# A new order of the steady batch on four engines, with odd layouts for denominators and block maxima

## The reference

```python
h = layernorm(x) * (1 + ca) + sa
x = x + ga * attention(h)            # 16 heads of 64, causal
h = layernorm(x) * (1 + cb) + sb
x = x + gb * ffn(h)                  # silu(gate) * up, then down, 352 hidden

# attention, per head
s = (q * scale) @ k.T
p = where(causal, 0, exp(s - max(s)))       # the max is taken before the mask
out = (p @ v) / (sum(p) + 1e-8)
# every ffn linear first rounds input and weight to FP4 in blocks of 16
scale = max(max(abs(block)) / 6, 1e-12)
q = GRID[searchsorted(MID, abs(block / scale))] * sign * scale
```

## Time and profile before

| | us |
|---|---|
| median of 3 runs | 1282.47 (1282.1 to 1282.92) |
| the profiled execution | 1283.31 |
| its span, first to last instruction | 1281.7 |
| mean granted TensorE clock | 0.993 of full |

### The profile page before, as it was taken

How to read it: one execution, slowest core, us unless ns; L and a number is a source line. 1 busy time by engine, 2 the same in 40 slices (tenths; PEclk the granted TensorE clock), 3 DMA queues, 4 the chain that set the end, 5 groups by cost and what they waited for, 6 DMA issues and landing times.

```text
span 1281.7 us, 34320 instructions
## 1 busy us (share of the span) xinstructions
PE 1247.3 (97%) x10194; PEld 1023.0 (80%) x10194; DVE 987.8 (77%) x2465; ACT 900.1 (70%) x2992; POOL 847.8 (66%) x1586
## 2 busy tenths in 40 slices
PE   6999999999999999999999999999999999999995
PEld 4778888888888888888888888788888788888774
DVE  5577877778777778777778777778787778787767
ACT  6676767776767777777777677777667777667761
POOL 4757666677666677666667666667666667666672
PEclk9999999999999999999999999999999999999997
DMA  3000000000000000000000000000000000000000
GB/s 105 20 20 24 18 7 23 23 23 23 13 9 23 23 23 22 10 13 23 23 23 21 9 15 23 23 23 21 6 18 23 23 23 20 6 18 23 19 21 9
DMA packets 38936, 26.53 MB, mean 21 GB/s; under 512 B 2912, under 2 KB 34144, under 8 KB 38912
## 3 DMA queue, kind: packets, MB, share of 16 engines
q1 hardware_dynamic: 38496, 25.96, 7.0%
q10 hardware_dynamic: 416, 0.26, 0.1%
HBM read 21.94 MB, written 4.28 MB: 20 GB/s over the span
## 4 chain that ended last, share of the span: by engine, by line
PE 95%; ACT 2%; DVE 2%; issue 1%; POOL 0%; DMA 0%; DVEq 0%; POOLq 0%
PE ps_m L1183 25%; PE ps_s L1282 20%; PE ps_m L1157 18%; PE ps_o L1312 14%; PE ps_m L1235 9%; PE ps_s L1292 5%; PE ps_m L1259 3%; ACT probs L688 1%; ACT qk L646 0%; PE ps_m L1403 0%; PE ps_s L1259 0%; ACT probs_t L642 0%; DMA x_in<-L_attn_x 0%; DVE neg_max L925 0%; DVE qy L62 0%
## 5 line engine op out<-in xcount | busy, mean ns | idle before, releaser
L688 ACT ACTIVATE probs<-ps_s,neg_max 128x128 f32<-128x128 f32 (+1 forms) x1024 | 424.2, 433 | 182.2 <-PE ps_s L1292 180.6
L467 POOL TENSOR_SCALAR probs<-probs,r_den 128x256 f32<-128x256 f32 (+1 forms) x768 | 355.4, 479 | 0.0
L925 DVE TENSOR_REDUCE neg_max<-ps_s 128x4 f32<-128x1024 f32 x256 | 305.6, 1215 | 61.0 <-PE ps_s L1282 61.0
L465 POOL TENSOR_TENSOR probs<-probs,r_den 128x128 f32<-128x128 f32 x256 | 107.5, 420 | 307.5 <-DVE r_den L936 293.3
L1282 PE MATMUL ps_s<-qk 64*128 64x256 f32 x2048 | 264.9, 394 | 1.8 <-ACT probs L688 1.8
L642 ACT COPY probs_t<-ps_m 128x512 f32<-128x512 f32 x287 | 167.8, 605 | 117.8 <-PE ps_m L1157 117.7
L1157 PE MATMUL ps_m<-ident,probs 128*128 128x128 f32 x1524 | 233.9, 277 | 5.4 <-ACT qk L646 3.6
L1282 PEld LDWEIGHTS ps_s<-qk 64*128 64x128 f32 x2048 | 183.0, 187 | 61.5 <-issue 32.4
L688 ACT ACTIVATION_READ_ACCUMULATOR probs<-ps_s,neg_max 128x1 f32 x1024 | 220.9, 216 | 0.0
L1157 PEld LDWEIGHTS ps_m<-ident,probs 128*128 128x128 f32 x1524 | 170.9, 140 | 38.0 <-ACT qk L646 13.3
L1312 PE MATMUL ps_o<-probs_t,v 128*64 128x256 f32 x2016 | 191.6, 332 | 0.7
(11 more groups left out here) (161 smaller groups left out, 1803.7 us busy)
## 6 DMA issues: line engine op xcount, KB each, us to landing
mod_a<-mod_rows SPq DMA_DIRECT2D x32, 256.0 KB, 3.3
x_res<-L_attn_x SPq DMA_DIRECT2D x32, 128.0 KB, 2.1
x_in<-L_attn_x SPq DMA_DIRECT2D x31, 128.0 KB, 2.1
out<-y_out SPq DMA_DIRECT2D x31, 128.0 KB, 1.8
mod_b<-mod_rows SPq DMA_DIRECT2D x31, 64.0 KB, 2.9
wkv<-L_attn_Wkv SPq DMA_DIRECT2D x3, 256.0 KB, 5.7
wo<-L_attn_Wo SPq DMA_DIRECT2D x1, 512.0 KB, 5.0
wkv<-L_attn_Wkv SPq DMA_DIRECT2D x2, 128.0 KB, 3.5
```

The lines of the kernel that those rows point to most:

```text
L465: nc.gpsimd.tensor_tensor(cols, cols, r_den[:, u % 4, 0:1].to_broadcast([P, P]), ALU.mult)
L467: ins = nc.gpsimd.tensor_scalar(cols, cols, r_den[:, u % 4, s:s + 1], 1.0, ALU.mult, ALU.mult)
L688: ins = nc.scalar.activation(probs[:, u % 4, h, t * P:(1 + 2 * t) * P], ps_s[:, 2 * (u % 2) + h, t * N:t * N + (1 + t) * P], ACT.Exp, bias ...
L925: nc.vector.tensor_reduce(neg_max[:, u % 4, :], ps_s[:, 2 * (u % 2):2 * (u % 2) + 2, :].rearrange("p b (t j) -> p (b t) j", t=2), AX.X, AL ...
```

## The change

Nothing is computed otherwise, but in another order and in part in other layouts. Each quarter's list changes on every engine:

- `SHARED`: some steps change places within their quarter. `v` number 2 goes from quarter 1 to 2, `down` number 0 and `hqt` number 1 from 2 to 3. There are still 36 steps, in three banks in turn.
- TensorE: masks stand at other places; after every `values` a mask comes first.
- ScalarE takes `t1` of quarter 0 and `t1` of quarter 1 and the `o_t` copy of quarter 3; VectorE takes `t1` of quarter 3 and the `o_t` copy of quarter 2.
- VectorE: the denominators of units 7 (of the batch before), 0 and 6 stand later in their quarters, `input_stats` in quarter 1.
- GpSimd: `keep` first in quarter 0, `residual` first in quarter 1, the second `round_hidden` at the end of quarter 2, `modulate` first in quarter 3.
- `den` has 9 columns per unit and `den_eps` 6; the eps addition reads 3 pairs with a stride of 3 and writes 6 columns. The hidden rows' block maxima are written in 11 pairs with a stride of 3 (`pair_scales`).
- The layer-norm result is made by `tensor_scalar` with two pointers in place of `scalar_tensor_tensor` with a broadcast second input.
- `den` is set to 1.0 by GpSimd at the start, and ScalarE waits for all eight set-up instructions before its first DMA.

```diff
+def pair_scales(nc, step, src, blocks, amax, scale, inverse):
+    pairs = amax[:, :].rearrange("p (a b) -> p a b", b=3)[:, :, 0:2]
+    step(nc.vector.tensor_reduce(pairs, src.rearrange("p (a b k) -> p a b k", b=2, k=BLOCK), AX.X, ALU.max,
+                                 apply_absolute_value=True))
+    step(nc.vector.tensor_scalar(scale[:, 0:blocks].rearrange("p (a b) -> p a b", b=2), pairs, 1.0 / 6.0, 1e-12,
+                                 ALU.mult, ALU.max))
+    step(nc.vector.reciprocal(inverse[:, 0:blocks], scale[:, 0:blocks]))
...
         SHARED = (
-            (("xqt", 2, 0), "t0", "qk0", "t1", "qk1", ("gate", 2, 0), ("v", 0, 0), ("v", 0, 1), "t2", ("up", 2, 0), ("gate", 2, 1)),
-            ("t0", "qk0", "qk1", ("up", 2, 1), ("wo", 1, 0), "t1", ("wo", 1, 1), ("hqt", 2, 0), "t2", ("v", 0, 2)),
-            (("hqt", 2, 1), ("down", 2, 0), "qk0", "t0", "qk1", "t1", ("v", 0, 3), ("xt", -1, 0), "t2"),
-            ("t0", "qk0", "qk1", ("down", 2, 1), "t1", "t2"))
+            ("t0", ("xqt", 2, 0), "qk0", "qk1", "t1", ("gate", 2, 0), ("v", 0, 0), ("up", 2, 0), ("v", 0, 1), "t2", ("gate", 2, 1)),
+            ("t0", "qk0", ("up", 2, 1), ("wo", 1, 0), "t1", ("wo", 1, 1), "qk1", "t2", ("hqt", 2, 0)),
+            ("qk0", "t0", ("v", 0, 2), "t1", "qk1", "t2", ("v", 0, 3), ("xt", -1, 0)),
+            ("qk0", ("hqt", 2, 1), "t0", "t1", ("down", 2, 0), ("down", 2, 1), "t2", "qk1"))
...
+            init(nc.gpsimd.memset(den[:, :, :], 1.0))
...
                 for j in range(PAIRS):          # GpSimd
                     if j == 0:
+                        keep()
                         normalize(i, -1)
                         normalize(i, 0)
                     elif j == 1:
-                        keep()
+                        residual()
                         normalize(i, 1)
-                        residual()
                         round_hidden(i - 2, 0)
                         normalize(i, 2)
-                        round_hidden(i - 2, 1)
                     elif j == 2:
+                        input_rstd()
                         attended_rstd()
-                        input_rstd()
                         normalize(i, 3)
                         normalize(i, 4)
+                        round_hidden(i - 2, 1)
+                    elif j == 3:
                         modulate()
-                    elif j == 3:
                         normalize(i, 5)
                         normalize(i, 6)
                         round_ffn_in()
...
+            act.wait_ge(pool_setup, POOL_SETUP)
             act.dma_start(x_in[:, :, :], x_v[0]).then_inc(x_loaded, 16)
...
-                    nc.vector.scalar_tensor_tensor(dst[t], src[:, t, :], mv[:, t, 0:1], r[:, t:t + 1].to_broadcast([P, P]),
-                                                   ALU.subtract, ALU.mult).then_inc(ready, 1)
+                    nc.vector.tensor_scalar(dst[t], src[:, t, :], mv[:, t, 0:1], r[:, t:t + 1], ALU.subtract, ALU.mult).then_inc(ready, 1)
...
-                    nc.vector.tensor_scalar(den_eps[:, u % 4, :], den[:, u % 4, :], SOFTMAX_EPS, None,
+                    nc.vector.tensor_scalar(den_eps[:, u % 4, :].rearrange("p (a b) -> p a b", b=2),
+                                            den[:, u % 4, :].rearrange("p (a b) -> p a b", b=3)[:, :, 0:2], SOFTMAX_EPS, None,
```

More of the change, by code:

```diff
@@ L178, in adaln_block @@
         qm = [sb(f"qm{n}", [P, I]) for n in range(3)]
-        amax = [sb(f"amax{n}", [P, I // BLOCK]) for n in range(3)]
+        amax = [sb(f"amax{n}", [P, 3 * I // BLOCK // 2]) for n in range(3)]
         scale = [sb(f"scale{n}", [P, I // BLOCK]) for n in range(3)]
@@ L734, in body @@
                         shared_reads(shared, j, 0)
[L735 removed]
                         shared_reads(shared, j, 1)
                         shared_reads(shared, j, 2)
+                        exponentials(6, 1)
                         exponentials(7, 0)
                         exponentials(7, 1)
[L740 to L741 removed]
+                        shared_reads(shared, j, 7)
+                        shared_reads(shared, j, 6)
+                        out_copy()
             high_parts(0)
@@ L984, in body @@
                         maxima(0)
-                        denominators(-1)
-                        shared_reads(0, 0)
-                        shared_reads(0, 3)
                         maxima(1)
@@ L990, in body @@
                             low_parts(2)
+                        out_copy()
+                        denominators(-1)
+                        shared_reads(0, 1)
                         shared_reads(0, 5)
-                        denominators(0)
-                        shared_reads(0, 8)
-                        shared_reads(0, 9)
-                        out_copy()
+                        shared_reads(0, 7)
                         hidden_scales(i - 2, 0)
                         shared_reads(0, 10)
+                        denominators(0)
@@ L998, in body @@
                     elif j == 1:
-                        denominators(1)
                         maxima(2)
                         maxima(3)
+                        denominators(1)
+                        input_stats()
                         hidden_magic(i - 2, 0)
+                        shared_reads(1, 2)
                         shared_reads(1, 3)
                         hidden_scales(i - 2, 1)
-                        shared_reads(1, 4)
+                        shared_reads(1, 5)
                         denominators(2)
-                        shared_reads(1, 6)
+                        if i_is(i, 1):
+                            shared_reads(1, 8)
+                    elif j == 2:
@@ L1008, in body @@
                         hidden_magic(i - 2, 1)
-                        if i_is(i, 1):
-                            shared_reads(1, 7)
-                    elif j == 2:
-                        input_stats()
+                        denominators(3)
+                        maxima(4)
                         attended_stats()
-                        maxima(4)
                         maxima(5)
-                        denominators(3)
-                        if i_is(i, 1):
-                            shared_reads(2, 0)
+                        out_copy()
@@ L1327, in body @@
                         at_place(0, 0)
+                        mask(0, 1)
                         at_place(0, 1)
-                        mask(0, 1)
                         at_place(0, 2)
@@ L1334, in body @@
                         at_place(0, 6)
+                        mask(1, 0)
+                        mask(1, 1)
                         at_place(0, 7)
                         at_place(0, 8)
-                        mask(1, 0)
-                        mask(1, 1)
                         at_place(0, 9)
@@ L1361, in body @@
                         at_place(2, 2)
+                        mask(5, 0)
                         at_place(2, 3)
                         at_place(2, 4)
-                        mask(5, 0)
+                        mask(5, 1)
                         at_place(2, 5)
-                        mask(5, 1)
                         at_place(2, 6)
                         at_place(2, 7)
-                        at_place(2, 8)
                     elif j == 3:
                         mask(6, 0)
-                        mask(6, 1)
                         at_place(3, 0)
                         at_place(3, 1)
+                        mask(6, 1)
+                        mask(7, 0)
                         at_place(3, 2)
+                        mask(7, 1)
                         at_place(3, 3)
-                        mask(7, 0)
                         at_place(3, 4)
-                        mask(7, 1)
                         at_place(3, 5)
+                        at_place(3, 6)
+                        at_place(3, 7)
             shared = shared_steps(-1)
-            for place in ((2, 7), (3, 1), (3, 2)):
+            for place in ((2, 7), (3, 0), (3, 7)):
                 kind, b, k, bank, _ = shared[place]
```

74 lines of the change are left out of this document (37 added, 37 removed).

## The result

The changed kernel is slower: a median of 1299.55 us (four runs, 1299.04 to 1299.78) against 1282.28 for the kernel before in the same comparison. The ratio is 1.0131, its 95% interval 1.0118 to 1.0145. The forecast was 1271.3 with a range of 1247 to 1290, so sign and range are both missed.

A forecast was written before the change was run, and what follows sets the result against it. TensorE's list plus its gaps bound the kernel: 1.25 us a batch out, 0.8 in, so 30 x 0.45 = 13.5 off 1283.31, start 2.35 on, 1272.2, adjusted by 0.84 to the median, 1271.3; range 1247 to 1290.

The forecast's parts named there:

- The removal: TensorE's waits in a steady batch: the new order takes out all of them, 1.25 us a batch.
- the nine gaps: TensorE's losses per batch: slow first scores block 0.3, four idle times 0.67 in all, four smaller ones 0.28.
- Step 3: Small new waits at quarter 0's second `v`, `xt` and unit 5's scores: 0 to 0.5 us a batch, taken as 0.25.
- step 1: Quarter 3, feed-forward input: `xq` comes late for `xqt` through `h2` and denominators 6; loss 0 to 0.4 us, taken as 0.3.
- step 2: Quarter 1, first transpose: waits for unit 0's late denominators and normalisation; 0 to 0.5 us, taken as 0.25.
- Step 5: Two-pointer normalising instructions on VectorE: 0.25 us each (bounds 0.175 to 0.83), 1 us less a batch on VectorE.
- Rival E: Two-pointer instructions wait for GpSimd: four take 1.9 us, `xt` up to 0.6 late, +0.15 a batch, 1289.3; chance 0.08.
- Rival D: Quarter 3: denominators 6 end later than 8.95 us into it, delaying `xqt`; 0.45 a batch longer, 1298.3; chance 0.12.
- Step 4: Odd layouts of denominators and hidden maxima avoid VectorE's wait for GpSimd; mostly off the path, 0 to 0.3 us a batch.
- Step 6: Start: ScalarE's first input DMA waits for eight set-up instructions and is issued at 3.1; +2.35 us (1.5 to 2.5).
- Step 7: SP: the output store and `mod_b` load move behind a later `y_out`; costs nothing.
- the tail: The end of the kernel: same hand-written end, change 0, within 1 us either way.

The follow-up runs named there:

- Experiment 15: As experiment 13, plus the first quotient instruction moved into VectorE's idle time and one hidden rounding instruction into GpSimd's; 1258.98 us, ratio 0.9814.
- experiment 12: As experiment 10, with GpSimd's second hidden rounding and modulation ahead of its normalisation of unit 4; 1280.29 us, ratio 0.9968.
- experiment 6: Changed kernel with GpSimd holding its second hidden rounding until both tiles of the next input are normalised; 1302.70 us, ratio 1.0144.
- experiment 5: Kernel before with only the two-pointer form of the four normalising instructions; 1282.02 us, ratio 0.9982.
- Experiment 4: Changed kernel with the old scalar_tensor_tensor in place of the two-pointer tensor_scalar; 1314.76 us, ratio 1.0248.
- experiment 10: Experiments 1 and 3 combined, with two quarter 3 reads ahead of the quotients, denominators 6 before the last read, keep behind unit 7; 1274.79 us, ratio 0.9930.
- experiment 11: As experiment 10, with one rounding instruction of the second hidden half moved into GpSimd's idle time in quarter 2; 1274.33 us, ratio 0.9925.
- experiment 13: As experiment 10, with the feed-forward input's rounding ahead of unit 6's normalisation on GpSimd; 1273.34 us, ratio 0.9923.
- Experiment 3: Changed kernel with the next input's tiles normalised ahead of the attended tiles on VectorE; 1287.90 us, ratio 1.0036.
- experiment 7: Changed kernel with the old dense layouts of denominators and hidden block maxima, and the earlier seven set-up constants; 1301.90 us, ratio 1.0138.
- experiment 1: Changed kernel with ScalarE's wait for GpSimd's set-up moved behind its first two DMA issues; 1294.17 us, ratio 1.0084.
- experiment 2: Kernel before with only ScalarE's wait for GpSimd's seven set-up constants put before its first transfers; 1288.77 us, ratio 1.0037.
- experiment 9: Experiments 1 and 3 combined, with VectorE's read of quarter 3's second transposes ahead of the quotients; 1292.08 us, ratio 1.0065.

## Why the prediction was wrong

- **The removal was right in kind and too large by 0.6.** All but small ones of the nine gaps went, and the first scores block fell to 2.00. Without its wait at `xt` the changed kernel would take 37.90 a batch (38.98 less 1.08), 0.65 under before, where the prediction took off 1.25. Experiment 15 has 37.85, 0.70 under before, with no idle time in the rows of PE. Whether another order gets the rest was not tried.
- **Step 3 failed, in the term "`xt` behind the two normalised tiles 0.1".** It is 1.08, and this one term turns the sign of the steady batches: 38.55 before, less the 0.70 of experiment 15, plus 1.08, is 38.93, and 38.98 was measured. By the rows all of it is hold-up beside GpSimd. The first of the four normalising instructions starts at 624.27, and `xt` was due at 625.42 (624.65 and 0.77). Four with nothing beside them take 1.11 (experiment 12); by that, an estimate, they would have ended at 625.38, in time. Here they took 2.18. No run has all four without hold-up in a steady batch. 0.62 of the loss went in experiment 6 with the rounding out of the way, and the other 0.46 stands beside the normalisation of unit 4.
- **The miss would have been larger without luck.** The removal was put 0.60 too high and steps 1 and 2 0.55 too high, and the two nearly cancel in the sum.
- **Step 5 gave the four a price that only holds with GpSimd idle beside them.** It took 0.25 us per instruction, "nearest to the plain rows". That is close to the 0.26 from start to start without hold-up, but none of the four runs so in a steady batch. Added up one by one they are 2.43 there. The row to go by was L849 itself, with 502 ns for `x` and 416 for `x_in`. That is 1.84 for four, 0.84 more than the prediction put, since most of L849's instructions are held beside GpSimd too (experiment 5).
- **The price of a neighbour was seen and put at the wrong instruction.** The earlier trace rows had it: 0.83 beside GpSimd's rounding. The prediction asked what would become of the scale there, and not what the new order puts beside the same rounding. GpSimd's `round_hidden` moved next to the last normalising instruction (0.98), and its first half next to the attended sum, L907: 0.93 where it took 0.29.
- **Rival E had this wait, and hung it on the two-pointer form.** It named GpSimd's normalisation of unit 4 as the neighbour, put the four at 1.9 and `xt` up to 0.6 late, and priced that at 0.15 a batch and a chance of 0.08. The neighbour was right for three of the four; the rounding beside the last one was not seen. Experiment 4 refutes the form: the old one is held too and is worse by 0.52 a batch. The Trainium skill, "Advanced Engine Details and Errata", section "VectorE Performance Modes", was cited for the form. The runs agree that the new instruction is held beside GpSimd, with 0.43 to 0.98 against 0.34. They do not bear out the line that the prediction drew between the two forms.
- **Rival D named the time, and not the cause.** 1298.3 against 1299.55 is chance. In the changed kernel denominators 6 end 8.2 into quarter 3 (634.92 and 0.18, from 626.87), under its 8.95, and `xqt` does not wait. D's chain behind denominators 6 became the limit only in experiments 10 to 13, with the waits ahead of it gone.
- **Steps 1 and 2 cost nothing, and not 0.55.** No idle time of a weight load stands at `xqt` or at quarter 1's first transpose. Step 1's walk was near all the same: from the start of quarter 3, `h2` is there at 3.3 (put at 4.0), denominators 6 at 8.2 (8.5) and `xq` at 12.2 (12.4 to 12.7, with a need put at 12.35). Quarter 3's chain of `h2`, quotients, reads and rounding was held off only by the gap before `xt`. Experiment 3 took that gap away and won 0.34 of its 1.08 us.
- **Step 4** was right: 0.09 a batch at most (experiment 7). Its reason is shown there too: beside the same GpSimd instruction the denominators take 0.83 in the dense layout and 0.16 in the odd one.
- **Step 6 failed in its size.** It moved the transfer by its issue, 2.35, and called the upper end 2.5; the first scores came 5.8 later and 4.6 to 5.4 of it reached the end (experiments 1 and 2). What was left out is that the transfer then stands among SyncE's, five of them issued by then, and takes 5.9 and not 2.4.
- **Step 7 and the tail:** nothing for step 7, as put, and 0.3 off in the tail.

## What to carry to other kernels

An order without gaps on paper is only as good as the durations in the new places. For each long instruction of GpSimd, list what VectorE does beside it in the new order, and price those pairs by rows, the same instruction's own row first; and look up what ran beside that row, since its mean may hold a hold-up already. When one wait goes, walk the next two or three in line on the same bank ring. Here four orders in a row (experiments 3, 9, 10 and 13) each uncovered the next one. The gain became real with the reads that free a bank in front of long arithmetic, GpSimd's rounding ahead of a normalisation, and part of the arithmetic put into idle time. A setup wait in front of a first transfer is paid with that transfer's place among the others.

## What the hardware showed

- A VectorE instruction that reads and writes SBUF can be held until just after the GpSimd instruction beside it ends. L862 with two pointers ends 0.08 after it: 0.34 with none beside it, 0.43 to 0.54 beside the normalisation (L479), 0.98 beside L83. Its older form ends 0.14 to 0.15 after. The sum L907 takes 0.93 beside L85 and 0.29 alone. GpSimd's own time hardly changes (0.92 to 0.97 in the rows shown): in these rows it is VectorE that pays.
- Not held in the same kernel were the scale and the denominators in the odd layout (0.18 and 0.16, with and without GpSimd beside them), the reciprocal behind the denominators (0.18) and the copy L872 out of PSUM (0.69). The changed kernel in quarter 1, with the held sum and the scale that is not:

```profile
613.77 0.94 POOL L85 TENSOR_TENSOR qy<-qy,qm 128x352 f32<-128x352 f32 x1
613.93 0.93 DVE L907 TENSOR_TENSOR x<-attn,x_gb 128x128 f32<-128x128 f32 x1
...
614.79 0.79 POOL L87 TENSOR_TENSOR hq<-qy,scale 128x352 f32<-128x352 f32 x1
615.32 0.18 DVE L64 TENSOR_SCALAR scale<-amax 128x22 f32<-128x22 f32 x1
```

- The same 128 KB transfer took 2.4 us when issued first, and 5.9 when issued 2.2 us later behind five others.
